# The opening of an f32 matmul chain on one core: the first weight piece in three transfers on two queues, and one warm-up matmul fewer

## The reference, cut to what matters

```python
# x: (8, 512, 2048); W: (2048, 2048); lora_As: (32, 2048, 16); lora_Bs: (32, 16, 2048); A: (8, 16, 2048)
y = einsum('bti,oi->bto', x, W) + b
y = y + einsum('btr,bro->bto', einsum('bti,bir->btr', x, lora_As[slot]), lora_Bs[slot]) * 2
logits = einsum('bsd,ed->bse', y, route_w)          # 8 experts, the best one is kept
out = x + einsum('bser,eor->bso', onehot(top1) * logit * einsum('bsd,erd->bser', y, A), Bw)
```

## Time and profile before

| what | value |
|---|---|
| median of 3 runs (lowest, highest) | 290.55 us (290.51, 290.59) |
| profiled execution, its own time | 290.62 us |
| span of its profile, first to last instruction | 288.8 us |
| TensorE busy in it | 283.0 us |

### The profile page before, as it was taken

The page is one execution under the profiler, slowest core; times in us unless marked ns, Lnnn a source line. Parts: engine busy times, 40 slices in busy tenths (PEclk is TensorE's granted clock), DMA queues, the critical chain, the costliest instruction groups (busy, mean ns, idle before and its releaser), DMA issues.

```text
span 288.8 us, 4485 instructions
## 1 busy us (share of the span) xinstructions
PE 283.0 (98%) x1734; PEld 226.9 (79%) x1734; DVE 203.2 (70%) x239; ACT 113.3 (39%) x171; POOL 12.9 (4%) x45
## 2 busy tenths in 40 slices
PE   8999999999999999999999999999999999999993
PEld 4999999996866885888588668857885887887993
DVE  0052200077697998799789969896997898898884
ACT  0001300295877523643373354427342732432500
POOL 6300030000000000000000000000000000000000
PEclk9999999999999999999999999999999999999999
DMA  6999999999980248759948993999499579555577
GB/s 238 409 406 396 402 415 412 374 415 422 420 372 3 111 182 287 295 197 411 379 179 310 407 371 147 365 378 349 154 397 387 228 258 414 203 218 238 201 248 263
DMA packets 19592, 88.54 MB, mean 307 GB/s; under 512 B 2410, under 2 KB 5106, under 8 KB 11762
## 3 DMA queue, kind: packets, MB, share of 16 engines
q1 hardware_dynamic: 16128, 84.87, 75.5%
q10 hardware_dynamic: 3442, 3.37, 3.6%
HBM read 54.60 MB, written 33.55 MB: 305 GB/s over the span
## 4 chain that ended last, share of the span: by engine, by line
PE 97%; DVE 1%; DVEq 0%; issue 0%
PE bank_out L635 16%; PE bank_h L710 11%; PE bank_h L711 10%; PE bank_h L712 10%; PE bank_e L695 10%; PE bank_out L673 10%; PE bank_out L675 10%; PE bank_out L674 10%; PE bank_h L642 1%; PE bank_l L649 1%; PE bank_l L635 1%; PE bank_r L635 1%; PE bank_e L635 1%; PE bank_h L635 1%; DVE x_ring L576 1%; PE bank_r L730 1%
## 5 line engine op out<-in xcount | busy, mean ns | idle before, releaser
L384 ACT ACTIVATE x_hi<-x_ring 128x1024 fp32r<-128x1024 f32 (+1 forms) x72 | 68.9, 965 | 64.9 <-PE bank_h L712 64.2
L482 DVE TENSOR_TENSOR x_lo<-x_ring,x_hi 128x1024 fp32r<-128x1024 f32 (+1 forms) x72 | 78.9, 1102 | 12.6 <-ACT x_hi L384 11.3
L576 DVE TENSOR_TENSOR x_ring<-bank_out,x_ring 128x1024 f32<-128x1024 f32 (+1 forms) x71 | 78.3, 1105 | 0.7 <-PE bank_out L675 0.3
L710 PE MATMUL bank_h<-x_hi,m_hi 128*128 128x512 f32 (+1 forms) x144 | 54.1, 376 | 0.0
L711 PE MATMUL bank_h<-x_lo,m_hi 128*128 128x512 f32 (+1 forms) x144 | 53.2, 369 | 0.0
L712 PE MATMUL bank_h<-x_hi,m_lo 128*128 128x512 f32 (+1 forms) x144 | 53.2, 369 | 0.0
L673 PE MATMUL bank_out<-wh_hi,bw_hi 128*128 128x512 f32 (+1 forms) x143 | 53.0, 370 | 0.0
L675 PE MATMUL bank_out<-wh_hi,bw_lo 128*128 128x512 f32 (+1 forms) x143 | 52.9, 370 | 0.0
L674 PE MATMUL bank_out<-wh_lo,bw_hi 128*128 128x512 f32 (+1 forms) x143 | 52.9, 370 | 0.0
L635 PE MATMUL bank_out<-pt,w_ring 128*128 128x136 f32 x384 | 46.0, 281 | 0.0
L635 PEld LDWEIGHTS bank_out<-pt,w_ring 128*128 128x128 f32 x384 | 45.4, 192 | 0.7 <-DMA w_ring<-W 0.7
(11 more groups left out here) (79 smaller groups left out, 165.0 us busy)
## 6 DMA issues: line engine op xcount, KB each, us to landing
x_ring<-xT SPq DMA_DIRECT2D x32, 1024.0 KB, 7.4
outT<-x_ring SPq DMA_DIRECT2D x28, 1024.0 KB, 4.8
w_ring<-W SPq DMA_DIRECT2D x30, 512.0 KB, 10.4
outT<-x_ring SPq DMA_DIRECT2D x12, 256.0 KB, 2.6
w_ring<-W SPq DMA_DIRECT2D x4, 256.0 KB, 4.6
x_ring<-loraB ACTq DMA_DIRECT2D x8, 128.0 KB, 10.2
la<-loraA ACTq DMA_DIRECT2D x8, 128.0 KB, 13.2
x_ring<-BwT SPq DMA_DIRECT2D x1, 1024.0 KB, 11.2
```

The costliest lines, as they stand in the source:

```text
L384: act.activation(out, in_, ACT.Copy).then_inc(done, 1)
L482: dve.tensor_tensor(out, a, b, ALU.subtract).then_inc(done, 1)
L576: dve.tensor_tensor(x, out_banks(u, j), x, ALU.add).then_inc(v_out, 1)
L710: mm(h, m_hi[:, c, :], hi, start=(c == 0), stop=False)
```

## The change

Piece 0 comes in three transfers. SP issues its chunk 0 and its chunk 1, 128 KB each; ScalarE's stream issues its chunks 2 and 3, 256 KB, after PT part 0 and ahead of PT part 1. TensorE waits for the three in turn. Piece 1 stays in two halves, now written through the same helper. The warm-up matmuls are eight instead of nine.

```diff
-    HALVED = 2
+    W_CUTS = {0: (1, 2), 1: (2,)}
...
-        d_w_first = [sem(f"d_w_first{n}") for n in range(HALVED)]
+        d_w_part = {(n, o): sem(f"d_w_part{n}_{o}") for n, cuts in W_CUTS.items() for o in cuts}
...
-        WARM_UP = 9
+        WARM_UP = 8
...
+        def load_w_part(eng, n, o0, o1):
+            blk, part = ORDER[n]
+            eng.dma_start(w_ring[:, n, o0:o1, :], W[blk, part, :, o0:o1, :]).then_inc(
+                d_w[n] if o1 == WO else d_w_part[n, o1], 16)
...
-                if n < HALVED:
-                    sp.dma_start(w_ring[:, n, 0:WO // 2, :], W[blk, part, :, 0:WO // 2, :]).then_inc(d_w_first[n], 16)
-                    sp.dma_start(w_ring[:, n, WO // 2:WO, :], W[blk, part, :, WO // 2:WO, :]).then_inc(d_w[n], 16)
+                if n == 0:
+                    load_w_part(sp, 0, 0, 1)
+                    load_w_part(sp, 0, 1, 2)
+                elif n in W_CUTS:
+                    load_w_part(sp, n, 0, 2)
+                    load_w_part(sp, n, 2, WO)
...
                 act.dma_start(pt[:, c0:c1, :], PT[:, c0:c1, :]).then_inc(d_pt[k], 16)
+                if k == 0:
+                    load_w_part(act, 0, 2, WO)
...
-                halves = ((0, WO // 2), (WO // 2, WO)) if n < HALVED else ((0, WO),)
-                for o0, o1 in halves:
+                cuts = (0, *W_CUTS.get(n, ()), WO)
+                for o0, o1 in zip(cuts, cuts[1:]):
...
-                        pe.wait_ge(d_w_first[n], 16)
+                        pe.wait_ge(d_w_part[n, o1], 16)
```

## The result

The change takes 291.85 us (median of 8, 291.59 to 293.56) against 290.41 (8 runs, 290.15 to 291.03): 1.44 us more by the medians, and 1.0062 times as long over all runs, 95% interval 1.0039 to 1.0085. Two of the eight runs stand apart, at 293.52 and 293.56, with a mean granted clock of 0.993 and 0.992; the other six lie at 291.59 to 292.13 with 0.996 to 1.0. The profile shown is one of the two.

What follows compares the result with a forecast made beforehand. TensorE alone was taken to set the time until 280 us; the 0.15 us won earlier lay inside the wait, so 290.62 + 0.36 = 290.98, put at 290.9 us against 290.55, range 290.3 to 291.3.

Steps and rivals of the forecast that it cites:

- What bounds the kernel: Whole kernel: only TensorE sets the time until 280 us, so opening time reaches the end one to one.
- One warm-up fewer: TensorE's opening: removes 0.42 us of work; at most 0.21 us come out, as work moved forward runs at half speed.
- rival D: TensorE's pause of about 0.15 us at 4.37 delays the clock's rise; outer bound 1.7 us lost, 292.3; chance 0.06.
- The first record at 4.53: First real matmul of line 635: starts 0.30 us earlier than 4.83, worth 0.15 us at full speed.
- The 0.3 us given to the small packets: PT part 0's landing: 1 KB packets of W beside it bring it in at 4.4 instead of 4.7 us.
- Chunks 2 and 3 ahead of PT part 1: ScalarE's queue: 8 more 2 KB packets ahead, with SP's turns, land PT part 1 at 6.5 instead of 5.7 us.
- 0.36 us lost: Ninth record, first past the wait for PT part 1: effectively 6.70 against 6.34 us.
- The turns themselves: DMA engines in the opening: the two queues take turns, packet for packet.
- The price of a 1 KB packet of W: DMA engines in the opening: 0.046 us, taken from the PT packet of 1088 bytes.
- The upper bound, 6.9: PT part 1's latest landing, 6.9 us, if half of the next SP transfer slips in front too.
- Chunks 2 and 3 themselves: ScalarE's queue: they land ahead of PT part 1, at about 5.5 us, and cost nothing.
- Piece 2 lands at 8.5 behind the same bytes as before: W's piece 2: wanted at 9.0 us, still there for a start 0.15 us earlier; costs nothing.

Runs made afterwards that it cites:

- e8: The change again, unaltered, for a second profile; 291.72 us.
- e2: The change's transfers with nine warm-ups instead of eight; 291.87 us.
- e5: The kernel before with eight warm-ups and nothing else changed; 290.27 us against 290.40.
- e1: The change with PT part 1 ahead of chunks 2 and 3 on ScalarE's queue; 292.2 us.
- e9: The change, but SP waits for chunk 1 to land before it issues piece 1; 292.26 us.
- e3: The change with all three transfers of piece 0 on SP's queue, PT parts 0 and 1 alone on ScalarE's; 290.73 us.
- e4: The change with PT part 1 moved to SP's queue, ahead of piece 1; 290.72 us.
- e7: The change with chunks 0 and 1 in one transfer of 256 KB instead of two; 293.13 us.
- e11: e4 with chunks 0 and 1 in one transfer, so 2 KB packets only; 290.42 us.
- e6: The change with nine matmuls on zeros filling TensorE's wait for PT part 1; six runs from 291.56 to 292.72 us.
- e12: The change with all of piece 0 on SP's queue, its first half cut by partitions (64 and 64, 2 KB packets); 292.4 us.
- e13: The kernel before with piece 0 as chunks 0 and 2, then 1 and 3 (1 KB packets), TensorE waiting for both; 291.5 us.
- e15: The kernel before with pieces 0 and 1 each as chunks 0 and 2, then 1 and 3 (1 KB packets); 291.66 us.

## Why the prediction was wrong

**What bounds the kernel: right.** The late ninth record came out at the end one to one: 1.13 us at the record, 1.2 in the span (e8).

**One warm-up fewer: right.** It costs nothing (e2, e5), and the pause in front of the first record, 0.22 us in e5, cost nothing in 12 runs (rival D where it was put). It also wins next to nothing.

**The first record at 4.53: right, a little too late**, 4.23 in the first profile and 4.38 in e8, and worth nothing, since it lies inside the wait. The 0.3 us given to the small packets was not too much: PT part 0 landed at 3.3 to 4.2 in the ten traces with 1 KB packets at the start, and at 4.3 to 4.7 in the six with 2 KB packets over 128 partitions. With eight warm-ups it was not the data but the end of the warm-up that set 4.37 or 4.38 in six of the ten.

**Chunks 2 and 3 ahead of PT part 1: the mechanism right, the size wrong, and this is the step that failed.** "PT part 1 is 0.74 us later: 5.7 + 0.74 = 6.4 ... I take 6.5" stands against 7.64 and 7.35 measured. e1, e9, e3 and e4 show that it is the queue's third place beside piece 1's turns. "0.36 us lost" was 1.13 to 1.43, and that makes +1.44 us out of the forecast +0.36. The turns themselves were as assumed: from 4.0 to 5.5 us 146 records of one queue passed beside 149 of the other (e8). The price of a 1 KB packet of W was nearly right too, 0.051 us for 0.046: from 2.33 to 3.30 us of e8, 155 records of SP's queue took 51.1% of the 16 engines' time, 0.511 x 16 x 0.97 / 155.

The upper bound, 6.9 "if half of the next SP transfer slips in front too", was too low as well. I took the price of a 2 KB packet from the kernel before and let it stand, while 0.110 us instead of 0.087 was paid per record of SP's queue in the change (e8). I had asked what a 1 KB packet costs itself, and not what it does to the packets behind it. I also mixed two stretches: 0.086 for W is from the first of the earlier trace rows, 0.046 for PT from the second, and in the first a PT packet took 0.410 x 16 x 0.97 / 87 = 0.073. At that price for the 1 KB packets the sum would have given 5.7 + 16 x 0.073 = 6.9, still too early. These rates don't account for all of the missing 0.9 us: e7, whose W packets are all of 2 KB or more, had 376 GB/s and PT part 1 still came 0.5 us after what the turns give, 5.7 + 1.4 = 7.1 against 7.6. A landing is the arrival of a transfer's last part, and a sum over mean packets gives a mean engine; how far the last of the 16 engines is behind was not measured, and where this part of the time went stays open.

Chunks 2 and 3 themselves landed at 1.19 + 3.9 = 5.1 and cost nothing, as forecast.

**Sound beyond PT part 1? Not quite.** "Piece 2 lands at 8.5 behind the same bytes as before": it landed at 2.59 + 6.5 = 9.1 in e8 and 2.59 + 6.8 = 9.4 in the first profile. In the change the late ninth record hides that; in e3 and e4, where piece 2 is also issued 0.47 us later, it lands at 9.7 and 9.4 and TensorE starts on it at 9.67 and 9.39 (e11: 8.88), which takes back what the earlier start won.

**Rival D: right in kind, wrong in place.** It was in the second pause, 2.38 us at the wait for PT part 1, that the clock fell, to 0.50 from 7.70 to 10.80 in the first profile, for 1.5 us more, near what I had put as an outer bound (1.7). One trace shows this and e6 supports it. I gave it to a pause of 0.15 us and never asked it of the pause that I forecast. The Trainium skill (TensorE: Matmul & The Clock Gate, Part 1: The HAM clock gate) has the chip look at TensorE's activity in windows that run on regardless of the kernel, so that where the rise falls depends on the run; the traces agree: the first 32 records take 4.45 us in the first profile of before (from 4.83; the earlier trace rows) and 4.56 in the second, 4.87 in e5, with no wait between records in any of them. The longer pause of e12 was followed by a late rise and that of e13 was not, one trace each; no run separates what a pause there does from this spread.

## What to carry to other kernels

Before a transfer is moved to a second queue, write down both queues side by side, and count what the other one spends its turns on while the moved one passes: needed data first on both queues (e4, e11) cost nothing that the runs can tell, needed data third beside data for later cost over 1 us. Ask of each forecast wait whether it is long enough to bring TensorE's clock down, since here that doubled its price in some runs. Don't cut W below 2 KB a partition in the opening for an earlier first byte: PT part 0 landed earlier by it (4.0 to 4.2 us instead of 4.3 to 4.7), but the piece of W that was wanted at 9.0 later (9.0 to 9.5 instead of 8.4 to 8.8).

## What the runs showed that I had not expected

A cut of the first pieces into 1 KB packets lowers what the DMA engines move right behind them by a fifth, from 361 to 289 GB/s on average from 4.0 to 5.5 us, at about the same busy share (0.92 to 1.10 without them, 0.98 to 1.05 with them). Twice as many small packets don't lower it further (282 and 308 GB/s, e13 and e15). Why the packets behind them take longer stays open. The spread of the kernel before itself, 289.92 to 291.37 over all these runs, is of the size of everything that the opening could win.
